# Four two-head maxima steps of layer 1 moved into the next sequence's scores, and three filler tiles moved up behind layer 0's maxima

## What is computed

```
q = heads(x @ Wq)                 k, v = heads(ctx @ Wk), heads(ctx @ Wv)
layer 0: out = softmax(q k_text) v_text + softmax(q k_ip) v_ip     text: 77 rows, ip: 298 rows
layer 1: p   = softmax(q k_text)  text_out = p v_text              text: 371 rows, ip: 4 rows
         sem = l2norm(p @ ctx_text) . l2norm(ctx_ip)
         ip_out = (softmax(q k_ip + 0.5 sem) * side) v_ip
out = (text_out + ip_out) @ Wout + b + x
```

## Time and profile before

| what | value |
|---|---|
| median of 3 runs | 2549.5 us (2545.89 to 2551.78) |
| the profiled execution | 2550.26 us |
| its span | 2548.5 us |
| TensorE's mean granted clock | 0.995 |
| busy share of the span | PE 96%, PEld 84%, DVE 64%, ACT 48%, POOL 30% |
| the chain that ended last | PE 77%, DVE 17%, SP's queue 2% |

### The profile page before, as it was taken

The page is one execution under the profiler, slowest core; times in us unless marked ns, Lnnn a source line. Parts: engine busy times, 40 slices in busy tenths (PEclk is TensorE's granted clock), DMA queues, the critical chain, the costliest instruction groups (busy, mean ns, idle before and its releaser), DMA issues.

```text
span 2548.5 us, 64247 instructions
## 1 busy us (share of the span) xinstructions
PE 2456.6 (96%) x26500; PEld 2137.2 (84%) x26500; DVE 1631.6 (64%) x3217; ACT 1226.4 (48%) x2251; POOL 768.5 (30%) x998
## 2 busy tenths in 40 slices
PE   7899999999999999999999999999999999999998
PEld 6788888888888888888888888888888888888877
DVE  4355667656667666677656677666676556676655
ACT  3354444455444554444554444554444544444543
POOL 2233233332233332333332332332332332332322
PEclk9899999999999999999999999999999999999999
DMA  8865456764456755466655466645566645566620
GB/s 210 138 91 90 93 89 98 107 100 85 88 90 102 117 83 90 83 94 112 104 80 87 84 107 102 110 74 89 98 95 106 91 86 88 88 98 102 95 28 18
DMA packets 373418, 241.47 MB, mean 95 GB/s; under 512 B 133675, under 2 KB 366971, under 8 KB 373116
## 3 DMA queue, kind: packets, MB, share of 16 engines
q1 hardware_dynamic: 373126, 237.36, 56.9%
HBM read 171.35 MB, written 64.59 MB: 93 GB/s over the span
## 4 chain that ended last, share of the span: by engine, by line
PE 77%; DVE 17%; SPq 2%; issue 1%; DMA 1%; ACT 1%; POOL 0%; DVEq 0%; POOLq 0%; ACTq 0%
PE ST L821 7%; DVE w L981 5%; PE R L887 5%; PE PN L860 5%; PE R L763 5%; PE R L776 4%; PE R L708 4%; PE R L777 4%; DVE m L1069 4%; PE R L709 4%; PE PN L905 3%; PE R L945 3%; PE R L779 3%; PE R L711 3%; DVE w L978 3%; PE R L890 2%
## 5 line engine op out<-in xcount | busy, mean ns | idle before, releaser
L1445 POOL TENSOR_TENSOR w<-w 128x448 f32<-128x448 f32 (+1 forms) x256 | 330.7, 1292 | 381.4 <-DVE w L978 363.2
L981 DVE SCALAR_TENSOR_TENSOR w<-p,pr 128x1344 f32<-128x1344 f32 x160 | 296.8, 1855 | 164.3 <-ACT pr L1331 151.0
L1303 ACT ACTIVATE p<-ST 128x1344 f32<-128x1344 f32 x260 | 335.5, 1291 | 104.1 <-PE ST L824 99.2
L887 PE MATMUL R<-pr,Gh 128*128 128x448 f32 (+1 forms) x960 | 366.2, 381 | 0.5 <-ACT pr L1331 0.5
L978 DVE TENSOR_TENSOR rem<-R,kst 128x298 f32<-128x298 f32 (+2 forms) x180 | 89.5, 497 | 426.4 <-ACT kst L1186 426.4
L978 DVE TENSOR_TENSOR w<-R,w 128x448 f32<-128x448 f32 (+1 forms) x480 | 281.5, 620 | 69.0 <-PE R L892 58.5
L1379 POOL TENSOR_TENSOR kst<-rem,kst 128x298 bf16<-128x298 f32 (+2 forms) x180 | 148.0, 822 | 533.9 <-ACT kst L1186 293.6
L776 PE MATMUL R<-wvh,ch 128*128 128x320 f32 (+3 forms) x896 | 302.6, 338 | 0.0
L777 PE MATMUL R<-wvh,cl 128*128 128x320 f32 (+3 forms) x896 | 277.0, 309 | 0.0
L821 PE MATMUL ST<-Qs,Ks 100*128 100x112 bf16 (+1 forms) x3520 | 228.6, 214 | 9.4 <-DMA Qs<-ms 2.7
L821 PEld LDWEIGHTS ST<-Qs,Ks 100*128 100x128 bf16 (+1 forms) x3520 | 187.7, 98 | 47.6 <-issue 13.4
(11 more groups left out here) (221 smaller groups left out, 5942.8 us busy)
## 6 DMA issues: line engine op xcount, KB each, us to landing
Ks<-k_split SPq DMA_DIRECT2D x384, 140.6 KB, 5.8
Ks<-k_split SPq DMA_DIRECT2D x384, 93.8 KB, 7.7
w<-in_ctxT SPq DMA_DIRECT2D x31, 750.0 KB, 9.8
k_split<-kst SPq DMA_DIRECT2D x64, 281.2 KB
k_split<-kst SPq DMA_DIRECT2D x64, 223.5 KB, 2.8
Qs<-q_split SPq DMA_DIRECT2D x64, 210.0 KB, 8.1
q_split<-qst SPq DMA_DIRECT2D x128, 84.0 KB, 2.4
Qs<-q_split SPq DMA_DIRECT2D x64, 140.0 KB, 8.2
```

Source lines behind the costliest of these rows:

```text
L887: e.matmul(r[0:nj, 0:QW], Gh[0:ROWS[u], q:q + nj], x[0:ROWS[u], QW * u:QW * u + QW], start=u == 0, stop=False)
L981: return e.scalar_tensor_tensor(out=to, in0=x, scalar=s, in1=y, op0=op0, op1=op1)
L1303: e.activation(to.rearrange("p (u q) -> p u q", u=3), st, ACT.Exp).then_inc(p_whole, 1)
L1445: e.tensor_tensor(first, first, w2[n % 2][0:ROWS[j], QW * j:QW * j + QW], ALU.add).then_inc(ns_added, 1)
```

## The change

The five lists of steps get names. For sequences 1 to 30 (`defers`) layer 1's maxima keep five steps (heads 0 to 11) in the maxima stretch, and heads 12 to 19 become four two-head steps in PN among the next turn's first two `scores` stages; `m_T` and `m_split` of layer 1 come two groups later, at g = 3 and 4. In the maxima stretch the fillers are drawn at counts 1, 3, 5, 6, 8, 9, 11, 13, so that three of them (`v_mm` of layer 1's third tile, the last Gram tile with its `split`, and a value tile of layer 0) come at counts 8, 9 and 11; and `rows0` is drawn from count 9 on. `m_T` now waits for all the steps that stand ahead of it in the list (`max_steps`).

```diff
+ALL_STEPS = [(h + d, n, d == 0) for h in range(0, H, 5) for d, n in ((0, 3), (3, 2))]
+NOW_STEPS = [(0, 3, True), (3, 2, False), (5, 3, True), (8, 2, False), (10, 2, True)]
+LATE_STEPS = [(h, 2, False) for h in range(12, H, 2)]
...
-    def maxima(b, l, between):
-        for h in range(0, H, 5):
-            for h0, wide in ((h, True), (h + 3, False)):
-                o.add("s_max", b, l, h0, wide)
...
+    def max_step(b, l, h0, n, wide):
+        key = (b, l, h0, n, wide)
+        o.add("s_max", *key)
+        for part in ("ST",) if wide else ("PV", "NS"):
+            o.share(part, 1, ("s_max", b, l, h0), "s_max_read", o.at("s_max", *key))
+
+    def maxima(b, l, steps, between):
+        for step in steps:
+            max_step(b, l, *step)
+            between()
         return m_rows(b, l)

     def m_rows(b, l):
         yield
+        o.max_steps[b, l] = o.many["s_max"]
         o.add("m_T", b, l)
...
+    def defers(b):
+
+        return SETS_FROM <= b + 1 < B
...
+        late = iter(LATE_STEPS if b and b < B and defers(b - 1) else ())
+
+        def late_step():
+            for step in islice(late, 1):
+                max_step(b - 1, 1, *step)
+
         def among0(g):
-            take(rows1, 1)
+            if b < B and defers(b - 1):
+                late_step()
+                take(rows1, 1 if g > 2 else 0)
+            else:
+                take(rows1, 1)
...
             take(pieces, 1 if b + 1 < B and (b or g < 4) else 0)
+            late_step()
...
             count[0] += 1
-            if count[0] > 9:
+            if count[0] > (8 if defers(b) else 9):
                 take(rows0, 1)
             if count[0] in (1, 2, 3, 5, 7, 9, 10):
                 take(last, 1)
-            if count[0] in (2, 4, 6, 8, 11, 12, 14, 16):
+            if count[0] in ((1, 3, 5, 6, 8, 9, 11, 13) if defers(b) else (2, 4, 6, 8, 11, 12, 14, 16)):
                 take(pieces, 1)
...
-            rows1 = maxima(b, 1, between)
+            rows1 = maxima(b, 1, NOW_STEPS if defers(b) else ALL_STEPS, between)
...
-                    w.wait_ge(s_max_read, 8 * at("m_T", b, l))
+                    w.wait_ge(s_max_read, o.max_steps[b, l])
```

More of the change, by code:

```diff
@@ L1 @@
 from contextlib import ExitStack
+from itertools import islice
 import concourse.bass as bass
@@ L37, in __init__ @@
         self.ring, self.slot, self.freed = {}, {}, {}
+        self.max_steps = {}
     def add(self, kind, *key):
@@ L335, in among @@
             warm("R", n)
-    rows0 = maxima(0, 0, among)
+    rows0 = maxima(0, 0, ALL_STEPS, among)
     flush()
@@ L425, in stage_order @@
         if b + 1 < B:
-            rows0 = maxima(b + 1, 0, between)
+            rows0 = maxima(b + 1, 0, ALL_STEPS, between)
             take(rows0, 1)
@@ L792, in tensor @@
                 elif kind == "s_max":
-                    b, l, h0, wide = key
-                    n, to = (3, ST) if wide else (2, PN)
+                    b, l, h0, n, wide = key
+                    to = ST if wide else PN
                     w.wait_ge(d_kr[l][0 if h0 + n <= HALVES[0][1] else 1], 96 * (b + 1))
```

## The result

The changed kernel takes 2817.98 us (median of 4 runs, 2812.36 to 2820.97) against 2549.15 for the kernel before: ratio 1.1055, 95% interval 1.1039 to 1.1072. It is 269 us slower. The forecast was 2837. The profiled execution took 2812.36 us, with a span of 2810.6 and a mean granted clock of 0.965, that is 262 more than the one of before.

A forecast was written before the change was run, and what follows sets the result against it. PE, busy 96%, was taken to bound the kernel. Maxima stretch 128, clock 72, scores stretch 88, last turn -0.6: together +287 on the profiled 2550.26, about 2837 us, own range 2800 to 2895.

The forecast's parts named there:

- POOL's split ahead of m_split: Maxima stretch: m_split queues behind the split on POOL, maxima land late; +4.4 us a turn, 128 us over 29 turns.
- The landing: Maxima stretch: the last of six DMAs lands 1.9 us after its issue, putting the maxima there at +29.2.
- The wait of m_T: Maxima stretch: m_T also waits for layer 1's first step's read, running at +16.0 (+15.5 to +16.1) instead of +13.63.
- The scores stretch: Moved heads +1.28, third late step's wait for DVE +1.35, layer 1's maxima +0.3 a turn; 88 us in 30 turns.
- The clock: After PE's 5 us pause at the scores the clock falls; 2.5 us a turn (0 to 2.95), 72 us over 29 turns.
- The two rows I sized it by: Earlier trace's low-clock stretches, 5.3 and 5.9 us at 0.50 after near-idle PE, each losing 2.65 and 2.95 us.
- The Trainium skill's figure: Clock loss by the skill page's example: 0.84 us a turn, 24 us in all, giving a sum of about 2789.
- That the clock stays up: Rival: the pause at the scores rarely or never lowers the clock, so 72 us fall away: 2765; chance 0.16.
- that POOL is in time: Rival: the maxima land before PE reaches the scores, so only the scores stretch costs: +70, 2620; chance 0.08.
- The one on the other side: Rival: DVE's reads pace the maxima stretch, so fewer reads there gain: -0.7 us a turn, 2528; chance 0.05.
- a pause of 2.3 us that left the clock up: Earlier trace, from 130.70: the clock stayed at 1.00 after this pause; cited for the rival without clock loss.

The follow-up runs named there:

- Experiment 1: The changed kernel with only the split of the context after next listed behind the maxima's m_split, so POOL runs m_split first: 2647.61 us, ratio 1.038.
- experiments 2 and 3: Changed kernel with m_T waiting only for layer 0's eight reads: 2780.32 us (2); the same plus split listed behind m_split: 2588.32 us (3).
- the fillers only: The changed kernel without late heads: fillers at their new places, all eight layer 1 steps back in the maxima stretch: 2713.81 us, ratio 1.065.
- the idle matmuls: The changed kernel with ten idle PE matmuls in the pause ahead of the scores, in turns that have a split: 2789.82 us, ratio 1.095.
- the late heads only: The changed kernel with fillers and rows0 at the counts of before, keeping the eight heads in the next scores stretch: 2699.39 us, ratio 1.059.
- experiment 7: The changed kernel without late heads, with split behind m_split and m_T waiting only for layer 0's eight reads: 2613.95 us, ratio 1.027.
- the last kernel: The kernel before with value and Gram tiles reordered and drawn earlier, o_mm later, layer 1's m_T one group later, no late heads: 2522.92 us, ratio 0.990.

## Why the prediction was right

**POOL's split ahead of m_split: right, in place and size.** I had `cl` at +18.7 to +22.25, `m_split` done at +23.45, the landing 1.9 behind the last issue at +29.2, PE there at +24.2, and the stretch 4.4 longer. The turn above has +18.88 to +22.41, +23.56, 1.85, +29.39 and +24.6; the 30 turns lost 135.8 where I had 127. Experiment 1 shows that the order is the cause. In turn 30, where I had a gain of 0.6, the stretch lost 1.6, since the clock fell behind `m_T`. The landing is a hit by luck. I took the lower of two bounds, from a row of another transfer, and gave as the reason that these are the smallest transfers. The list of the kernel before has smaller ones, loaded once, and they took longer (KB, then us to landing):

```profile
mip_sb<-in_mip SPq DMA_DIRECT2D x1, 0.5 KB, 7.4
...
side<-in_side SPq DMA_DIRECT2D x1, 0.4 KB, 5.6
```

**The wait of m_T: right, a little short.** +16.32 against +16.0, outside my upper end of +16.1. Without the wait for layer 1's step it is +14.94 (experiments 2 and 3). So the rule costs 1.38, and layer 0's own reads come 1.31 later than before (+13.63), where I had 0.5 and 0.4 for them: that part was too small.

**The scores stretch: right.** I had 88 for work and waits, 2.93 a turn in 30 turns. The two kernels with late heads in which the clock stayed up in every scores stretch (experiments 1 and 3) lost 87.3 and 85.9 in 29 of them, 3.0 a turn. The parts were a little off against each other: DVE's wait is 1.2 on average (I had 1.35), the wait for layer 1's maxima 0.4 (I had 0.3). Layer 1's `m_T` and `m_split` come three groups later (g = 3 and 4, before 0 and 1), not two.

**The clock: right that it falls, the term too large.** I took 2.5 a turn in 29 turns, 72. Of the 127.8 in the scores stretch some 41 are left when those 87 are taken off. It fell in 24 of the 29 scores stretches behind such a pause, and cost 41 / 24 = 1.7 each. Behind the pause above (length, then PE, PEld, DVE, ACT, POOL, granted clock):

```profile
640.60:644.20 3.60, 0.00 (x0) 0.00 (x0) 0.00 (x0) 0.00 (x0) 0.00 (x0) 1.00 0.06 12
644.20:647.00 2.80, 2.73 (x20) 2.64 (x21) 1.00 (x2) 1.29 (x1) 0.00 (x0) 0.58 0.43 115
647.00:650.00 3.00, 2.48 (x22) 2.21 (x21) 0.91 (x3) 0.90 (x2) 0.04 (x1) 0.82 0.00 0
```

2.80 x 0.42 + 3.00 x 0.18 = 1.72 is lost. The two rows I sized it by the earlier trace rows were low for 5.3 and 5.9 us; here the low stretch ends sooner. So the term is 31 too large, and against it stand 9 more in the maxima stretch; that is most of why the profiled execution lost 262 and not 287. That the forecast is only 19 us off owes something to these two errors of opposite sign. The Trainium skill's figure (page "TensorE: Matmul & The Clock Gate", section "HAM oscillation — how this bites in real kernels"), 0.84 a round by its example, would have made it 24 us, an estimate from that page. The trace lies between that and the two rows.

**The rivals.** That the clock stays up fell with those rows, that POOL is in time with POOL's rows. The one on the other side, that DVE's reads were the bound and fewer of them are a gain (layer 1 has three steps less there, not four), is true of the maxima stretch: with the two late causes repaired it is 1.6 shorter than before (23.24 against 24.80). It fell on its condition that the late steps fit into the scores stretch without a wait; they cost 3.0 a turn there, the moved work included.

## What to carry to other kernels

In a list that orders every engine at once, moving a filler for PE moves all its followers: look for the longest operation that it puts ahead of a short one with a deadline, on engines that look idle (here POOL, busy for 30%: 3.6 us ahead of 1.2 us, 170 of 269 us). The engine need not even be working: POOL stood idle for 1.9 us with `m_split` ready, because `cl` was ahead of it and still waited for ACT. A wait for "everything so far" changes when the order changes; let it count what it needs. And work taken from a crowded stretch costs more than its own time where it is put, if its reader is queued behind another chain there (here 3.0 us a turn for 1.28 us of work).

## What was not expected of the hardware

**One pause, two outcomes.** PE's pause ahead of `m_T`, with the same 1.58 us of idle time in its row each turn, was followed by the lower clock in 14 turns of 30 and left it up in 16. The change, behind `m_T` of turn 5 and of turn 6:

```profile
545.00:547.00 2.00, 2.00 (x16) 2.00 (x15) 0.00 (x0) 0.79 (x4) 0.00 (x0) 0.67 0.00 0
547.00:549.00 2.00, 2.00 (x5) 1.25 (x5) 1.27 (x3) 1.95 (x6) 1.16 (x2) 0.50 0.04 8
...
631.00:633.00 2.00, 1.80 (x18) 1.79 (x19) 0.06 (x1) 0.84 (x5) 0.00 (x0) 1.00 0.00 0
633.00:635.00 2.00, 2.00 (x10) 1.34 (x9) 1.29 (x4) 1.90 (x6) 1.24 (x2) 1.00 0.00 0
```

In the change that costs little where PE waits for the maxima anyway (all turns but the last): it comes to the scores 1.0 to 1.7 later and waits that much less, and the 13 such stretches with a fall took 29.6 on average, the 16 without 29.4. In experiment 1 it is the 26.3 against 24.62. I had read from a pause of 2.3 us that left the clock up that such short ones do no harm; the earlier trace rows has the pause itself, and the row behind it, of the kernel before, is

```profile
133.00:136.00 3.00, 3.00 (x38) 2.92 (x38) 0.00 (x0) 1.99 (x4) 0.00 (x0) 1.00 0.00 0
```

One pause of the start of the kernel was too little to read that from. Other kernels have the two outcomes too. The same 1.58 us ahead of `m_T` was followed by the lower clock in 10 of 30 turns in experiment 1, in 16 with the fillers only and in 13 with the idle matmuls; 2.22 us in 14 of 30 with the late heads only. In experiment 7 a pause of 0.86 us ahead of the scores, with one of 0.57 shortly before, was followed by it in 14 of 29, and from turn 6 to turn 27 in a strict order, two turns with a fall and two without. The 0.65 us ahead of `m_T` in the last kernel left it up in all 30. What decides between the two outcomes no run here shows.
